# The third head's sums in the graph attention layers of a three-layer graph network: formed by TensorE in PSUM and weighed from there

## The reference

```python
xl = (x @ Wl + bl).reshape(n, h, d)
xr = (x @ Wr + br).reshape(n, h, d)
e = jax.nn.leaky_relu(xl[src] + xr[dst], NEG_SLOPE)
score = jnp.einsum('ehd,hd->eh', e, att)
m = jax.ops.segment_max(score, dst, num_segments=n)
ex = jnp.exp(score - m[dst])
denom = jax.ops.segment_sum(ex, dst, num_segments=n)
alpha = ex / denom[dst]
out = jax.ops.segment_sum(alpha[:, :, None] * xl[src], dst, num_segments=n)
```

## Time and profile before

| | |
|---|---|
| median of 3 runs | 7210.68 us (7207.19 to 7213.8) |
| profiled execution | 7218.68 us |
| its span, first to last instruction | 7216.6 us |
| busy: DVE, PE, POOL, ACT | 83%, 73%, 55%, 51% of the span |
| edge loop of GATv2 layer 1 | from about 2277 us to 3901 us |
| edge loop of GATv2 layer 2 | from about 4123 us to 5746 us |

### The profile page before, as it was taken

One profiled execution on the slowest core, in us unless ns is written; L12 is line 12 of the kernel. 1 busy time (PEld: TensorE's weight loads), 2 busy tenths in 40 slices (PEclk: granted clock), 3 DMA queues, 4 the chain that ended last, 5 costly groups with the idle time before them and its releaser, 6 DMA issues. The chain is left out here.

```text
span 7216.6 us, 134164 instructions
## 1 busy us (share of the span) xinstructions
PE 5244.3 (73%) x20244; PEld 3043.4 (42%) x20245; DVE 6002.7 (83%) x16763; ACT 3700.4 (51%) x17817; POOL 3953.3 (55%) x3546
## 2 busy tenths in 40 slices
PE   3544444499956889898988789898989846566663
PEld 2444433133323444444445444444444435555552
DVE  9766657799965999999998499999999855777776
ACT  5111113300014999999996399999999831000000
POOL 0688888860002666666662166666666405777773
PEclk9999999899978999999999899999999967777775
DMA  0465664000013555555553255555555404444443
GB/s 11 78 78 79 78 72 50 1 1 0 0 33 125 139 140 140 139 140 139 140 137 64 90 140 140 139 139 138 140 140 139 91 19 120 126 125 125 125 125 68
DMA packets 440612, 705.63 MB, mean 98 GB/s; under 512 B 146470, under 2 KB 315464, under 8 KB 440146
## 3 DMA queue, kind: packets, MB, share of 16 engines
q0 software_dynamic: 185888, 481.62, 26.2%
q1 hardware_dynamic: 254642, 223.19, 15.7%
HBM read 668.31 MB, written 33.88 MB: 97 GB/s over the span
## 5 line engine op out<-in xcount | busy, mean ns | idle before, releaser
L1173 POOL DMA_INDIRECT feat_area<-xl_table,feat_area x1856 | 2002.6, 1079 | 2120.9 <-issue 1196.4
L1324 ACT ACTIVATE feat_area<-feat_area 128x130 f32<-128x130 f32 x5568 | 1644.5, 297 | 216.9 <-DVE feat_area L1377 214.8
L1234 PE MATMUL bank<-node_area,feat_area 128*128 x3712 | 1472.2, 520 | 357.8 <-DVE feat_area L1369 193.9
L1308 ACT ACTIVATE feat_area<-feat_area 128x128 f32<-128x128 f32 x4640 | 1441.8, 387 | 0.0
L1247 PE MATMUL bank<-feat_area 128*128 128x390 f32 x3712 | 1410.6, 503 | 18.0 <-DVE feat_area L1391 4.2
L564 POOL DMA_INDIRECT rec_by_dst<-feat_area,gather_col x800 | 1059.1, 1324 | 248.9 <-issue 223.1
L1736 POOL DMA_INDIRECT feat_area<-kv_table,feat_area x832 | 839.9, 1009 | 561.5 <-DMA feat_area<-gather_src 306.7
L1234 PEld LDWEIGHTS bank<-node_area,feat_area 128*128 128x128 f32 x3712 | 636.2, 191 | 1005.9 <-issue 752.7
L1324 ACT ACTIVATION_READ_ACCUMULATOR feat_area<-feat_area 128x1 f32 x5568 | 1040.3, 187 | 0.0
L1247 PEld LDWEIGHTS bank<-feat_area 128*128 128x128 f32 x3712 | 673.0, 191 | 584.5 <-issue 172.8
L1369 DVE TENSOR_TENSOR feat_area<-bank,feat_area 128x780 f32<-128x780 f32 x928 | 885.8, 955 | 28.6 <-DMA feat_area<-xl_table,feat_area 27.8
(11 more groups left out here) (294 smaller groups left out, 7291.5 us busy)
## 6 DMA issues: line engine op xcount, KB each, us to landing
feat_area<-lo_slot SPq DMA_DIRECT2D x464, 128.0 KB, 3.3
node_area<-in_dst SPq DMA_DIRECT2D x200, 250.0 KB
feat_area<-xl_table,feat_area POOLq DMA_INDIRECT x1856, 3.4
feat_area<-lo_slot_src SPq DMA_DIRECT2D x208, 128.0 KB, 3.3
node_area<-lo_edge SPq DMA_DIRECT2D x200, 125.0 KB
xl_table<-feat_area SPq DMA_DIRECT2D x98, 195.0 KB, 2.2
feat_area<-kv_table,feat_area POOLq DMA_INDIRECT x832
rec_by_dst<-feat_area,gather_col POOLq DMA_INDIRECT x800
```

Of the source, the lines that this page charges most:

```text
L1173: pool.indirect_dma_start(ring[:, at:at + HE], None, k.xl, bass.IndirectOffsetOnAxis(ap=index[s // CG][:, n:n + 1], axis=0)).then_inc(gath ...
L1234: last = nc.tensor.matmul(pair[s % 2][:, u, 0:HE], pick[s // 2 % 2][:, c:c + P], k.node[:, ds(columns[0], HE)], start=True, stop=True)
L1308: last = nc.scalar.activation(row[:, 0:D], row[:, 0:D], ACT.Copy, scale=row[:, D:D + 1])
L1324: last = nc.scalar.activation(at, at, ACT.Copy, accum_out=score[s // CG][:, to:to + 1])
```

## The change

Three things, all in `gat_edges`. `L = 2 * 130 = 260` marks where the third head's columns begin.

In `look`, PE, after its two lookup matmuls of a group, waits for that group's gathers and adds the third head's gathered rows (130 columns of each of the two tiles) onto the looked-up ones in PSUM, by two more matmuls with the identity. In `add`, DVE adds only the first two heads (2 x 260 columns), and a second instruction reads the third head's finished sums from PSUM, takes the larger of 0 and them, and multiplies by the attention vector into `z`. `weigh` then covers the first two heads alone. Waits of `sums`, of the gathers and of ACT are as before.

```diff
+    L = (H - 1) * DW
...
                 for u in range(GS):
                     c = (s % 2 * GS + u) * P
-                    last = nc.tensor.matmul(pair[s % 2][:, u, 0:HE], pick[s // 2 % 2][:, c:c + P],
-                                            k.node[:, ds(columns[0], HE)], start=True, stop=True)
+                    nc.tensor.matmul(pair[s % 2][:, u, 0:HE], pick[s // 2 % 2][:, c:c + P],
+                                     k.node[:, ds(columns[0], HE)], start=True, stop=True)
+                pe.wait_ge(gathered[s], 16 * GS * j + 16 * GS)
+                for u in range(GS):
+                    at = s * W + u * HE
+                    last = nc.tensor.matmul(pair[s % 2][:, u, L:HE], k.ident[:, :], ring[:, at + L:at + HE],
+                                            start=False, stop=True, skip_group_check=True)
                 last.then_inc(looked, 1)
...
-                nc.vector.tensor_tensor(z[s % V].rearrange("p (u e) -> p u e", u=GS), pair[s % 2][:, :, 0:HE],
-                                        ring[:, s * W:(s + 1) * W].rearrange("p (u e) -> p u e", u=GS), ALU.add
-                                        ).then_inc(added, 1)
+                zu = z[s % V].rearrange("p (u e) -> p u e", u=GS)
+                nc.vector.tensor_tensor(zu[:, :, 0:L], pair[s % 2][:, :, 0:L],
+                                        ring[:, s * W:(s + 1) * W].rearrange("p (u e) -> p u e", u=GS)[:, :, 0:L], ALU.add)
+                nc.vector.scalar_tensor_tensor(out=zu[:, :, L:HE], in0=pair[s % 2][:, :, L:HE], scalar=0.0,
+                                               in1=att_w[:, L:HE].unsqueeze(1).to_broadcast([P, GS, DW]),
+                                               op0=ALU.max, op1=ALU.mult).then_inc(added, 1)
...
-                zu = z[s % V].rearrange("p (u e) -> p u e", u=GS)
-                nc.vector.scalar_tensor_tensor(out=zu, in0=zu, scalar=0.0, in1=att_w.unsqueeze(1).to_broadcast([P, GS, HE]),
+                zu = z[s % V].rearrange("p (u e) -> p u e", u=GS)[:, :, 0:L]
+                nc.vector.scalar_tensor_tensor(out=zu, in0=zu, scalar=0.0,
+                                               in1=att_w[:, 0:L].unsqueeze(1).to_broadcast([P, GS, L]),
                                                op0=ALU.max, op1=ALU.mult).then_inc(weighed, 1)
```

## The result

| | median, us | range | 
|---|---|---|
| before | 7210.83 | 7207.19 to 7213.8 (4 runs) |
| after | 7902.74 | 7895.82 to 7914.4 (4 runs) |

The ratio is 1.0962 (95% interval 1.0948 to 1.0976): 692 us slower. The direction was forecast, the size (+448) was too small, and the time lies 73 us above the range. Outside the two edge loops nothing changed (3970 us before, 3976 after). From the first lookup to the end of the last sums, layer 1's loop went from 1624 to 1978 us and layer 2's from 1623 to 1947.

What follows compares the result with a forecast made beforehand. DVE was taken to bound the edge loops at 3.43 us a group. A chain of 3.93 us would replace it: (3.93 - 3.43) x 896 = +448 us, 7666.7 us, or 7658.7 on the median's scale; range 7450 to 7830 us.

Steps and rivals of the forecast that it cites:

- What bounds before, DVE's part: Edge loops: DVE bounds at 3.43 us a group; its add and weigh fall from 1.77 to 1.57 us.
- the bound of -111: Edge loops: ACT's unchanged work keeps a group at 3.31 us or more, a gain of at most 111 us.
- The loop of two groups: Sums of g - 16, gathers of g, identity of g, sums of g - 14: 3.93 us a group sets the pace.
- the term for the gathers' issues: POOL's two gathers behind the sums: first issue 1.18 us, second near the 0.947 us median.
- The rule on two SBUF inputs: Gather issues under DVE's weigh: a shorter weigh takes a few hundredths off the 1.18 us, some 20 us in all.
- Four passes of 130 columns: PE's identity matmuls: 0.49 us from the first start to the start of what follows.
- Chunk work, 0.04 us a group: PE, one step in eight: two transposes of 51 columns, 0.205 us each, stand between identity and sums.
- the landing: Second gather's arrival: median 3.5 us from start of issue, least 3.0, most 5.1; 5.76 us after the sums' end.
- A gain: Rival: gathers come in time, a group takes ACT's 3.31 us, -111 us, 7100 us; chance 0.04.
- The clock's fall: Rival: PE's pauses lower its clock to 0.73, its 3.5 us become 4.8, +1230 us, 8440 us; chance 0.03.
- PE as the bound: Rival: PE's 3.5 us or a chain up to 3.70 us a group sets the pace, +60 to +242 us; chance 0.09.
- The low end's 1.9 us: Low bound's time behind the landing: 5.02 + 1.9 = 6.92 us for two groups, 3.46 per group, +27 us.

Runs made afterwards that it cites:

- the relief alone: The changed kernel without the identity matmuls and PE's wait, third head's gathered rows left out of its scores: 7667.89 us, ratio 0.9887.
- the kernel without the loop: Changed kernel without PE's wait, identity matmuls reading a constant: 7836.78 us, 3.52 us a group; kernel before plus four constant passes: 7232.58 us, 3.44.

## Why the prediction was off in size

- **What bounds before, DVE's part.** Right. 520 columns took 0.687 us (forecast 0.684), 260 out of PSUM 0.415 (0.413), and the relief alone stopped near ACT's pace, -91 us against the bound of -111.
- **The loop of two groups.** Right in mechanism. PE waited for gathers in most groups, the wait alone cost +492 us, moving it behind the sums left +39.
- **The step that failed is the term for the gathers' issues**: "The second of a pair is near the median, so the first is 2 x 1.07 - 0.96 = 1.18 us." In the trace of before the firsts took 1.14 us in the mean and the seconds 1.01, because of where DVE's weigh stood at a pace that DVE set. In the changed kernel the sums' end starts both the gathers and DVE's step, so the two are locked: firsts take 0.95 us, the odd groups' seconds 1.42. By durations alone that is (0.46 - 0.23) / 2 = 0.12 of the 0.28 us a group that were missed; the run that moved the weigh shows 0.19 us a group (176 us), the clock and the landings with it. The forecast let this term only fall, by some 20 us. With the weigh moved the pace is 4.02 us, near the forecast of 3.93.
- **The rule on two SBUF inputs.** The Trainium skill (SBUF — State Buffer, Who interferes with whom) says that a VectorE instruction with two SBUF inputs contends with a GpSimd one that reads SBUF. The trace agrees: the 780-column weigh held issues before, the 520-column one holds them still (1.45 us in the mean of 348). I used it to take off 20 us for a shorter weigh, and didn't ask which issue it would lie on. The rows carried it: the issue that began at 3007.94 ended at 3009.31, 0.82 us after the weigh, so what counts is how far into the issue the weigh reaches, and not how long the weigh is.
- **Four passes of 130 columns** took 0.55 us from their first start to the sums' (3006.08 to 3006.63), against 0.49 forecast from the node layer's rows. The formula that the forecast set beside it is what the Trainium skill (TensorE: Matmul & The Clock Gate, Back-to-back issue gap) calls the isolated gap; for a stream of weight loads and matmuls it has about 81 ns at 128 columns. The trace agrees with neither: its float32 passes start 0.11 us apart.
- **Chunk work, 0.04 us a group.** Its own terms, 2 x 0.205 us in one step of eight, give 0.05; the transposes took 0.82 - 0.55 = 0.27 us in one odd group of four, 0.03 a group. That term holds. The odd groups' tail behind the landing was 2.39 us against 2.10 all the same: of the 0.29 us, 0.14 are sums at the low clock, 0.09 rows that wait for PE. In the kernel with the weigh moved the clock's part is gone and 8.04 us stand against 7.86. There the rows wait 0.32 us for PE, against 0.05 forecast; why, and so the last 0.09 us a group or 80 us, stays open.
- **The rivals.** A gain didn't come. The clock's fall did, in small and beside the loop, not in its place: 0.97 and 0.99 where it was 1.00, far from 0.73, and worth 0.07 us a group in layer 1. The forecast had no term for it. PE as the bound was the right price for the kernel without the loop: 3.44 to 3.52 us against "3.35 to 3.55".
- **The range.** Its ends came from the spread of one link, the landing, which hardly moved (2.58 against 2.54), while the issues were taken at their means. (The low end's 1.9 us behind the landing is 2.02 by its own terms.)

## What to carry to other kernels

A new wait on an in-order engine has to be asked what stands behind it and who waits for that: here the transfers that it waits for were themselves waiting for the work behind it, and a loop over two groups closed, although the transfers had been early for every consumer until then. The same wait behind that work, 1.5 us later in the step, cost 22 to 39 us in place of 692. When the pace changes hands from one engine to a loop, phases between engines lock anew, so issue times that depend on a neighbour should be taken from the new phase, at both ends, and not from the old mean.

## What the runs showed of the hardware

- A gather's issue that begins under the weigh, a VectorE instruction with two SBUF inputs, lasts until about the weigh's end plus 0.8 us: 1.48 us for one that began at 3010.13 under a weigh ending at 3010.79, 0.82 us behind the end in the mean of 348 such issues, and 0.84 in the mean of 379 in the kernel before. The 789 that began there under the add, with one input in PSUM, took 0.95 us. Another VectorE instruction follows the same figure with one SBUF tensor and a column as its scalar: 227 issues that began under the making of `pick` (L1354) ended 0.82 us behind it.
- Exchanging two VectorE instructions of 0.69 and 0.42 us was worth 176 us, where the gathers' loop sets the pace.
- With PE's waits for the gathers (in 2600 to 3600 us up to 2.8 us for matmuls, 3.5 for weight loads) the granted clock there was 0.97 instead of 1.00, 0.96 with the wait alone, so for some 6 to 8% of the time TensorE ran at 1.2 GHz. Between groups 120 and 440 of layer 1 it did so 20 times, and the sums there took up to 2.97 us instead of 1.48. With the weigh moved, and waits of up to 2.1 and 2.7 us, the clock stayed at 1.00.
